# A decoder layer on one core: another order of its tensors in SBUF, and one group of its feed-forward part moved ahead of a query projection

## What is computed

```python
x = _layernorm(x + _L0_attn_ref(x, W_Q, W_K, W_V, W_out, b_out), axis=-1)
x = _layernorm(x + _L0_xattn_ref(x, ctx_1024, ln_w, ln_b, Wq, Wkv, Wout, mask, 5), axis=-1)
x = _layernorm(x + _L0_ffn_ref(x, w_gate, w_up, w_down), axis=-1)
```

## Time and profile before

| | |
|---|---|
| three runs | 2037.02, 2037.97, 2039.48 us; median 2037.97 |
| the profiled execution | 2038.91 us, of which the span is 2037.1 us |
| PE busy | 2008.3 us, 99% of the span |
| DVE, ACT, POOL busy | 1545.8, 1322.5, 375.3 us |
| granted TensorE clock, mean | 0.996 |

### The profile page before, as it was taken

One profiled execution on the slowest core, in us unless ns is written; L12 is line 12 of the kernel. 1 busy time (PEld: TensorE's weight loads), 2 busy tenths in 40 slices (PEclk: granted clock), 3 DMA queues, 4 the chain that ended last, 5 costly groups with the idle time before them and its releaser, 6 DMA issues.

```text
span 2037.1 us, 50598 instructions
## 1 busy us (share of the span) xinstructions
PE 2008.3 (99%) x18176; PEld 1845.4 (91%) x18176; DVE 1545.8 (76%) x5708; ACT 1322.5 (65%) x3992; POOL 375.3 (18%) x624
## 2 busy tenths in 40 slices
PE   8999999999999999999999999999999999999997
PEld 7899999999999999999999999999999999999886
DVE  6877777777777777777777777777777777777764
ACT  8866666667666666666666666666666666666642
POOL 3112111211211111112121112112121211121121
PEclk9999999999999999999999999999999999999998
DMA  5100000000000000000000000000000000000000
GB/s 163 32 8 22 18 22 12 11 19 19 22 12 19 11 19 22 18 12 22 8 21 19 12 22 8 22 18 22 12 19 11 19 22 19 12 11 19 13 7 11
DMA packets 49606, 41.19 MB, mean 20 GB/s; under 512 B 19536, under 2 KB 47568, under 8 KB 49360
## 3 DMA queue, kind: packets, MB, share of 16 engines
q1 hardware_dynamic: 49360, 37.96, 6.4%
HBM read 29.56 MB, written 8.39 MB: 19 GB/s over the span
## 4 chain that ended last, share of the span: by engine, by line
PE 95%; DVE 1%; ACT 1%; DMA 1%; issue 1%; POOL 0%; SPq 0%; POOLq 0%; DVEq 0%; ACTq 0%
PE gen L441 20%; PE gen L442 19%; PE gen L443 19%; PE s_ps L581 9%; PE z_ps L623 7%; PE gen L529 3%; PE pt_ps L602 3%; PE gen L538 3%; PE gen L542 3%; PE pt_ps L603 3%; PE pt_ps L607 3%; PE z_ps L625 3%; PE gen L509 2%; PE gen L500 1%; PE gen L553 1%
## 5 line engine op out<-in xcount | busy, mean ns | idle before, releaser
L954 ACT ACTIVATE SM<-SM,least 128x128 f32<-128x128 f32 (+1 forms) x1024 | 452.2, 447 | 35.2 <-DVE least L1479 35.1
L884 ACT ACTIVATE PT<-pt_ps 128x512 f32<-128x512 f32 (+1 forms) x512 | 237.5, 485 | 239.7 <-PE pt_ps L603 237.4
L1479 DVE CUSTOM_DVE_ANT_0 SM<-s_ps,causal 128x128 f32<-128x128 f32 (+1 forms) x1024 | 314.7, 352 | 19.2 <-PE s_ps L581 14.3
L1492 DVE TENSOR_SCALAR SM<-SM,total 128x128 f32<-128x128 f32 (+1 forms) x1024 | 282.3, 339 | 9.0
L1858 POOL TENSOR_TENSOR H_lo<-gated,H_hi 128x256 fp32r<-128x256 f32 x192 | 141.7, 745 | 517.6 <-ACT H_hi L884 517.5
L937 ACT ACTIVATE gated<-gen 128x256 f32<-128x256 f32 x192 | 73.6, 383 | 202.6 <-PE gen L443 202.5
L581 PE MATMUL s_ps<-KT,QT 64*128 64x128 f32 (+1 forms) x2048 | 201.5, 336 | 1.4 <-ACT KT L884 0.7
L954 ACT ACTIVATION_READ_ACCUMULATOR SM<-SM,least 128x1 f32 x1024 | 196.1, 192 | 0.0
L1456 DVE SCALAR_TENSOR_TENSOR gated<-gated,gen 128x256 f32<-128x256 f32 x192 | 80.9, 421 | 120.5 <-ACT gated L937 120.1
L623 PE MATMUL z_ps<-PT,Vt 128*64 128x256 f32 x1024 | 168.1, 399 | 0.0
L581 PEld LDWEIGHTS s_ps<-KT,QT 64*128 64x128 f32 x2048 | 147.7, 187 | 21.7 <-issue 6.4
(11 more groups left out here) (185 smaller groups left out, 6507.8 us busy)
## 6 DMA issues: line engine op xcount, KB each, us to landing
xT_in<-in_xT SPq DMA_DIRECT2D x32, 256.0 KB, 2.9
x_in<-in_x SPq DMA_DIRECT2D x32, 256.0 KB, 2.8
out<-rows SPq DMA_DIRECT2D x32, 256.0 KB, 2.2
ctx_in<-in_ctxT SPq DMA_DIRECT2D x32, 77.0 KB, 2.8
mask_in<-in_maskT SPq DMA_DIRECT2D x32, 77.0 KB, 2.6
SX<-in_wq SPq DMA_DIRECT2D x1, 512.0 KB, 6.3
rows<-in_wv SPq DMA_DIRECT2D x1, 512.0 KB, 7.4
xwk<-in_xwkv SPq DMA_DIRECT2D x1, 512.0 KB, 8.1
```

Of the source, the lines that this page charges most:

```text
L884: return act.activation(o, i, ACT.Copy)
L954: ins = act.activation(part, part, ACT.Exp, scale=-1.0, bias=least[:, i % 4, n:n + 1], accum_out=total[:, i % 4, n:n + 1])
L1479: ins = dve.tensor_tensor_reduce(SM[:, i % 4, at:at + keys], s_ps[bank][:, col:col + keys], causal[:, S - keys:S], -SCALE, -3 * NEG, ALU.a ...
L1492: ins = dve.tensor_scalar(part, part, total[:, i % 4, n:n + 1], None, ALU.mult)
```

## The change

It does two things. It puts the SBUF tensors in another order. And in full turns it swaps `fFFN5` and `aQ3`: on PE `fFFN5` comes straight after `transposed(a, 2)`, then `aQ3`, then `oXQ1`; on ACT `fFFN5` and `aQ3` both come ahead of `exps(4, 1)`; on DVE `fFFN5` comes ahead of `masked(5, 1)`. The first and last turns keep their order.

```diff
 ITEMS = [
-    "fFFN3", "oT10", "oT11", "fFFN4", "aQ3", "fFFN5", "oXQ1", "oXQ0", "oSIM10", "oSIM11", "oSIM00", "oSIM01",
+    "fFFN3", "oT10", "oT11", "fFFN4", "fFFN5", "aQ3", "oXQ1", "oXQ0", "oSIM10", "oSIM11", "oSIM00", "oSIM01",
...
         wk_s = halves("wk", [P, KD, KE])
-        wv_s = halves("wv", [P, KD, KE])
-        wo_s = halves("wo", [P, NP, D])
         xwq_s = halves("xwq", [P, KD, XE])
-        xwk = sb("xwk", [P, KD, XE])
-        xwv_s = halves("xwv", [P, KD, XE])
-        xwo_s = halves("xwo", [P, XP, D])
         wg_s = halves("wg", [P, KD, HID])
         wu_s = halves("wu", [P, KD, HID])
+        den = sb("den", [P, T, 2, XH])
+        wv_s = halves("wv", [P, KD, KE])
+        xwv_s = halves("xwv", [P, KD, XE])
+        least = sb("least", [P, 4, 4])
+        wo_s = halves("wo", [P, NP, D])
+        xwo_s = halves("xwo", [P, XP, D])
         wd_s = halves("wd", [P, KH, D])
+        xT_s = halves("xTs", [P, KD, S])
+        NX_s = halves("NX", [P, KD, S])
+        NT_s = halves("NT", [P, KD, S])
+        total = sb("total", [P, 4, 4])
+        Z_s = halves("Z", [P, NP, S])
+        H_s = halves("H", [P, KH, S])
+        xwk = sb("xwk", [P, KD, XE])
...
 # PE, turn_between
                 t.transposed("a", 2)
+                t.fill("fFFN5")
                 t.fill("aQ3")
-                t.fill("fFFN5")
                 t.fill("oXQ1")
                 t.transposed("a", 3)
...
 # ACT, turn_between
                 t.exps(4, 0)
+                t.fill("fFFN5")
                 t.fill("aQ3")
                 t.exps(4, 1)
-                t.fill("fFFN5")
                 t.probs_out("a", 2, 1)
...
 # DVE, turn_between
                 t.nx_low_out()
+                t.fill("fFFN5")
                 t.masked(5, 1)
-                t.fill("fFFN5")
```

More of the change, by code:

```diff
@@ L207, in decoder_layer @@
         xT_in = sb("xT_in", [P, KD, S])
-        xT_s = halves("xTs", [P, KD, S])
         QT = sb("QT", [P, 2, 2, S])
@@ L212, in decoder_layer @@
         SM = sb("SM", [P, 4, PAIR])
-        least = sb("least", [P, 4, 4])
-        total = sb("total", [P, 4, 4])
         PT = sb("PT", [P, 2, PAIR])
-        Z_s = halves("Z", [P, NP, S])
         rows = sb("rows", [P, 2 * T * D])
@@ L225, in decoder_layer @@
         Y = XN_t
-        NX_s = halves("NX", [P, KD, S])
-        NT_s = halves("NT", [P, KD, S])
-        H_s = halves("H", [P, KH, S])
         ones = sb("ones", [P, 1])
@@ L246, in decoder_layer @@
         pmax = sb("pmax", [P, T, 3, XH])
-        den = sb("den", [P, T, 2, XH])
         QX = sb("QX", [P, XH * P])
```

## The result

The changed kernel takes 2047.71 us (median of five runs, 2047.20 to 2049.10) against 2038.93 us of five runs of the kernel before beside it; the ratio is 1.0047, with a 95% interval of 1.0036 to 1.0058. It is slower, by 8.8 us; 2046 was forecast. The profiled execution is the median one: 2047.71 us, 8.80 above the 2038.91 of the profile before.

A forecast was written before the change was run, and what follows sets the result against it. PE's own stream of matmul pitches was taken to bound the kernel. 2038.91 + 21.5 (wait) - 12.8 (layout) = 2047.6 us profiled, 2046.7 for the median, put at 2046; range 2028 to 2061.

The forecast's parts named there:

- the layout term: Projections' fp32r streams: distance 192 throughout makes more matmuls run at 113.3 instead of 117.8 ns, saving 12.8 us.
- The wait at pair 3: PE's transpose of pair 3 waits for ACT's copy of PT: 0.74 us a turn, 21.5 us; chance of no wait 0.10.
- the extra pitch at the restart: PE's first pitch after a wait is 0.19 us instead of 0.12, 0.07 more, since weights were not loaded ahead.
- XQ1's wait for FFN5's bank: PE starts XQ1 0.28 us late; this lies inside the wait at pair 3 and adds nothing.
- a share of 0.61 short: After the change 0.61 of 264 matmuls run at the short pitch, 161 against 72 before, saving 0.40 us a batch.
- the count of 23 starts: Of 23 starts of 256-column streams at distance 192 in the old trace, 14 settled at 113.3 ns, giving the share.
- a short stream stays short through fills of the same distance: On PE, a stream once at 113.3 ns keeps that pitch through following fills with equal operand distance.
- they repeat one luck 29 times: Full turns all settle their streams alike, so the same short or long pitches recur in all 29.
- All long: Bound of the layout term: every matmul at 117.8 ns, a loss of 10.4 us; within a rival of chance 0.22.
- The rule on ports: The skill's statement that PE reads streaming and loaded operands through independent ports; by it the layout term is 0.
- Values, T1 and XPV: Rival: values and XPV slow down at distance 0, up to 7 us, giving 2053 us; chance 0.05.
- What the view would show: PE waits in a full turn: 0.5 to 0.6 us each for PT, 29 times, and 0.2 us at XQ1.

The follow-up runs named there:

- copy_first: Changed kernel with ACT's second copy out of pt_ps of pair 2 moved ahead of Q3's copy and exps(4, 1): 2036.63 us, 0.9997 of the kernel before.
- swap_only: Kernel before with the swap of Q3 and FFN5 alone, its SBUF order kept: 2057.59 us, 1.0093 of the kernel before.
- last run: New SBUF order and old order of work, with least moved ahead of wv so V has distance 0, all others 192: 2031.82 us, 0.9968.
- layout_only: The changed kernel's SBUF order with the order of work of the kernel before: 2030.78 us, 0.9966 of the kernel before.

## Why the prediction was right

The range, the sign and the sum held. The wait came as its chain was written; the layout term came out near its size partly by luck.

- **The wait at pair 3.** Forecast 0.74 us a turn, 21.5 us; measured 0.70, 20.2 us, and 0.69, 20.0 us, with the swap alone. The chain was ACT's queue as written: 0.32 from Q3's last start to its copy (forecast 0.31), 0.50 to `exps(4, 1)` (0.50), 0.88 to the copy (0.87), 0.37 for the copy (0.38), 0.14 until PE starts (0.14). The copy_first run shows that these two calls were all of it. Too large was the extra pitch at the restart: 0.13 against 0.11 for a transpose, 0.02 where 0.07 was taken from a restart of fp32r matmuls.
- **XQ1's wait for FFN5's bank**, forecast 0.28 and hidden inside the other: XQ1 came 0.14 late and lost 0.10 more in its first pitch (0.22 for 0.12), 0.24. Hidden it was; in copy_first, with the cover gone, it is the 0.22 us that stays.
- **The layout.** Forecast 12.8 us, from a share of 0.61 short; measured 9.20 - 20.2 = -11.0 us in full turns, -0.4 outside, with a share of 178 / 276 = 0.64. Two errors in it work against each other: 106 matmuls more than before were short, not 89, and each brought 3.6 ns on the mean (11.0 us / 29 / 106) and not 4.5, since a stream that settles short starts long and XQ1's nine save nothing. The size is right by more luck than the count of 23 starts deserved: with the old order of work the same layout had 125 / 276 = 0.45 and gained 7.0 us. The prediction took the share as a property of the distance alone, and it belongs to the starts as well. That a short stream stays short through fills of the same distance held in the new layout and failed at DOWN in swap_only. What it said of the full turns, that they repeat one luck 29 times, was too strict: Q0, K0 and DOWN changed from turn to turn.
- **The bounds.** "All long" at 117.8 ns was the lower end of what a distance can do. For 192 it may be; other distances go down to 120.0, so a layout term of the wrong sign could have been far larger than the 10.4 us that I allowed.
- **The rule on ports.** Where the loaded operand lies against the streaming one does set the pace: the same operands and counts ran at 113.3 to 120.0 ns by their distance alone. The Trainium skill ("TensorE: Matmul & The Clock Gate", Step-by-step: what each phase is for) has the streaming and the loaded operand read through ports of their own, so that a load takes nothing from the stream; by it the layout term was 0, and the trace doesn't agree. What the two reads have in common, no run shows.
- **Values, T1 and XPV** went from 128 to 0 and I allowed them up to 7 us. They cost nothing: a row of sixteen value matmuls took 1.50 us before and after, T1's two segments 0.27 and 0.31 us both times, XPV's 0.88 and 1.02 (means of 25 turns). The SIM fills went from 0 to 128, which the prediction left out, and took 0.92 and 0.98 us both times. That rival fell.
- **What the view would show.** Forecast were waits of 0.5 to 0.6 us at `PT` and of 0.2 at XQ1; shown were 0.29 and none. The losses were there and the reading of the view was wrong: idle time counts from the end of a record, which is 0.16 us behind the next start that could have been (0.28 less 0.12).

What stays open: what in a start settles a stream at 113.3 or 117.8 ns. The runs show that the distance weighs in, that the state survives from fill to fill without a break in the new layout (FFN0 to FFN2; Q0, K0 and DOWN together) and is lost between K0 and DOWN in the old one (swap_only), and that a change ahead of a start can flip it (FFN3 in the last run, Q0 in copy_first). None shows a rule that foretells a given start.

The best version here is layout_only: 2030.78 us, 0.9966 [0.9953, 0.9978] of the kernel before, and 0.8% below the changed one. The layout was the good half of the change and the swap the bad half.

## What to carry to other kernels

When an engine's queue is reordered, write out what each call waits for and who waits behind it: a copy that PE needed stood behind a call that couldn't start yet, the swap cost 20 us, and moving that one line won 11 us back. When PE is busy all the time, price a change by the starts of its matmuls, not by busy and idle time: here +20 and -11 us showed as 8.3 us of idle time and an unchanged busy time. And when fp32r streams run back to back, lay the operands out on purpose and try the distances; spacers of some bytes moved this kernel by 1.6% between the worst distance (2064 us) and the best (2031), with 2038 before.

## What was unexpected of the hardware

- The pitch of an fp32r stream of 256 columns with a load of 128 beside each matmul depends on the addresses of its two operands modulo 256 bytes: 113.3 to 120.0 ns at full clock, in steps of 32 bytes not monotonic. A common shift of 96 bytes changed nothing.
- At 64 and at 192 two stable pitches exist, 113.3 and 117.8 ns. A stream can keep the short one across fills, for 84 matmuls from FFN0 to FFN2 in the new layout; between K0 and DOWN in swap_only it was lost, at the same distance and without a break. A stream that settles short runs its first three or four pitches longer (FFN4: 120, 117, 116, 114 ns behind the restart).
- Streams of 512 columns order the distances in another way: their segment of twelve was shortest at 0 (2.83 us), 2.86 at 64 and 2.87 to 2.89 elsewhere.
